# One matmul per group of keys stands half a loop step earlier on TensorE: graph network kernel, first edge stage

## The reference

```
h = relu(layernorm(x)); x = x + L0(h)   # segment sum of edge_attr_32 by src, two dense layers, batch norm
h = relu(layernorm(x)); x = x + L1(h)   # gather features[src], message per edge, scatter-add by dst
h = relu(layernorm(x)); x = x + L2(h)   # 3 rounds: segment_sum(norm * out[row], col), clipped
h = relu(layernorm(x)); x = x + L3(h)   # 3 rounds: segment_sum(wn * z[src], dst), relu, batch norm
```

## Time and profile before

| | us |
|---|---|
| median of 3 runs | 3483.51 |
| lowest and highest run | 3475.79, 3485.16 |
| the profiled execution, its own time | 3486.41 |
| its span in the profile | 3484.7 |
| first stage in it, first turn to last matmul | about 82 to 1006 |
| POOL's first add, last add, first gather | 222.06, 1021.88, 1058.52 |

### The profile page before, as it was taken

The page is one execution under the profiler, slowest core; times in us unless marked ns, Lnnn a source line. Parts: engine busy times, 40 slices in busy tenths (PEclk is TensorE's granted clock), DMA queues, the critical chain, the costliest instruction groups (busy, mean ns, idle before and its releaser), DMA issues. The chain is left out here.

```text
span 3484.7 us, 69264 instructions
## 1 busy us (share of the span) xinstructions
PE 2978.0 (85%) x19702; PEld 2385.9 (68%) x19703; DVE 2742.2 (79%) x5981; ACT 2291.3 (66%) x3192; POOL 2104.3 (60%) x1629
## 2 busy tenths in 40 slices
PE   3788788888877999999999999999999976657656
PEld 3677677777766888888888888888888841114256
DVE  6678888888877999999999999999999973450064
ACT  3678587877847888888888888888888832230000
POOL 4037888888866777777777777777777720000000
PEclk9999799899988999999999999999999987798878
DMA  9953222222213333333333333333333369999830
GB/s 402 422 188 36 12 15 16 14 15 15 15 6 67 52 50 52 52 52 50 52 52 51 52 52 52 50 52 52 51 51 52 52 242 426 425 389 377 362 139 6
DMA packets 265841, 397.89 MB, mean 114 GB/s; under 512 B 149901, under 2 KB 200836, under 8 KB 259252
## 3 DMA queue, kind: packets, MB, share of 16 engines
q0 software_dynamic: 149184, 124.54, 21.1%
q1 hardware_dynamic: 100180, 199.71, 16.9%
q10 hardware_dynamic: 16416, 72.92, 5.1%
HBM read 264.96 MB, written 132.05 MB: 114 GB/s over the span
## 5 line engine op out<-in xcount | busy, mean ns | idle before, releaser
L577 POOL DMA_INDIRECT both<-kept x782 | 1295.9, 1657 | 443.4 <-issue 205.1
L916 PEld LDWEIGHTS ps<-prod,big 128*128 128x128 f32 x7840 | 1134.3, 190 | 136.8 <-DVE prod L1283 133.2
L916 PE MATMUL ps<-prod,big 128*128 128x170 f32 x7840 | 1183.2, 310 | 22.2 <-DVE prod L1283 16.7
L585 POOL DMA_INDIRECT kept<-feat_dram,kept x782 | 760.8, 973 | 279.8 <-issue 232.2
L907 PE MATMUL ps<-prod,onehot 128*128 128x320 f32 x3920 | 719.4, 339 | 133.5 <-ACT onehot L665 116.2
L660 ACT ACTIVATE big<-iota_b,kept 128x640 f32<-128x640 f32 x1029 | 779.0, 815 | 13.6
L907 PEld LDWEIGHTS ps<-prod,onehot 128*128 128x128 f32 x3920 | 639.6, 207 | 167.9 <-issue 121.1
L665 ACT ACTIVATE big<-big 128x2560 f32<-128x2560 f32 x196 | 458.1, 2337 | 275.3 <-PE ps L916 275.2
L981 PE MATMUL ps<-w2mix,kept 65*128 65x384 f32 x1568 | 559.3, 500 | 21.6 <-ACT kept L712 21.6
L1455 DVE TENSOR_REDUCE kept<-kept 128x80 f32<-128x1280 f32 x392 | 562.0, 1474 | 0.0
L981 PEld LDWEIGHTS ps<-w2mix,kept 65*128 65x128 f32 x1568 | 284.1, 191 | 179.7 <-issue 23.5
(11 more groups left out here) (232 smaller groups left out, 2988.8 us busy)
## 6 DMA issues: line engine op xcount, KB each, us to landing
both<-big POOLq DMA_DIRECT2D x40, 2000.0 KB, 96.2
big<-both SPq DMA_DIRECT2D x50, 1600.0 KB, 10.7
adj_w<-kept ACTq DMA_DIRECT2D x32, 800.0 KB, 33.3
big<-adj_w SPq DMA_DIRECT2D x32, 800.0 KB, 12.1
big<-adj_w ACTq DMA_DIRECT2D x32, 800.0 KB, 11.7
kept<-keys_dram SPq DMA_DIRECT2D x196, 128.0 KB, 3.0
kept<-in_wT SPq DMA_DIRECT2D x196, 128.0 KB, 3.0
adj_c<-kept ACTq DMA_DIRECT2D x42, 400.0 KB, 32.5
```

Of the source, the lines that this page charges most:

```text
L577: pool.indirect_dma_start(both, bass.IndirectOffsetOnAxis(ap=sc_idx[:, c:c + 1], axis=0), sc_val[:, c // 2, c % 2, :], None, compute_op=AL ...
L585: pool.indirect_dma_start(gath[:, s % 2, k, :], None, feat_dram, bass.IndirectOffsetOnAxis(ap=src_i[:, 4 * s + k:4 * s + k + 1], axis=0)). ...
L916: mm = pe.matmul(part_sums(part, MSG), onehot[:, q, k, part * P:(part + 1) * P], prod[:, q, k, 0:HI * MSG], start=False, stop=False, skip_ ...
```

## The change

`spread_keys` for the next group but one stands in the even step, between the step's second and third chunk behind the hop, where it was in the odd step behind `merge_open`. It is the same 98 matmuls with the same two waits; the group's number and its slot are the same as well, only the place is one step earlier. No other engine's instructions move.

```
@@ phase0 on PE @@
                     merge_hop(g, slot, 2)
                 elif not is_last(s):
                     merge_open(g, slot)
-                if k4 % 2 and not is_last(s, 4):
-                    spread_keys(g + 1, 1 - slot)
+                if k4 % 2 == 0 and not is_last(s, 4):
+                    spread_keys(g + 2, slot)
                 scatter0(s, k4, 2)
                 scatter0(s, k4, 3)
```

## The result

The change made the kernel no faster: median 3492.18 us (20 runs) against 3482.40 us before (20 runs), ratio 1.0025 with a 95% interval of 1.0016 to 1.0034. Forecast were 3453 us. The single times spread more than before: 3478.15 to 3502.60 us, against 3475.79 to 3488.98. The profiled execution is the shortest of its twenty, 3478.15 us with a span of 3476.4 us; a second profile, of an execution of 3497.36 us, stands with the experiments.

The account below looks back on a forecast made before the run. A cycle of waits among PE, ACT and DVE paced the first stage. Its 43 us gain met POOL's limit, 34.8 - 3 - 1 = 31 us: 3486.4 - 31 = 3455.4, adjusted for the profiled run's 2.9 us above median to 3453; range 3446 to 3470.

Parts of the forecast that it names:

- the one at the seam: Where the first stage's adds end and the second stage's gathers begin: adds lengthen by 3 us in all.
- The cap: POOL's queue of first-stage adds, ahead of the first gather, limits the whole gain to 31 us; chance 0.60.
- The sign that the prediction had named for this: First-stage adds on POOL taking over 2.1 us each would show the forecast limit on the gain to be wrong.
- The 1 us in the same sum: At the second stage's start: 1 us taken off the gain for the first gather's data behind the adds.
- The ring is cut: First stage: the earlier spread ends ACT's waits for it, 0.88 and 2.31 us in the turn read.
- The added wait at nothing: PE's spread, now in the even step, waits for ACT's earlier squares: no cost, 1.6 us away from biting.
- The moved spread hidden by PE's wait for products: Even step on PE: the spread's 0.31 us cost nothing; at most 30 us without that cover.
- The clock: First stage: PE clock falls, 2.5 us each, drop from 0.47 of the turns to a fifth.
- The stage's gain: First stage: 37.5 turns become shorter by 43 us in all, at least 18 and at most 62 us.
- the clock as before: Rival, first stage: PE clock falls as often, gain 18 us, 3465 us; with cases between, 3456 to 3470, chance 0.25.
- The new wait: Rival, even step: PE held for ACT's squares, 41 us slower, 3525 us; chance 0.08 together with more clock falls.
- Nothing happens: Rival, first stage: DVE's turn stays at 17.48 us, its instructions lengthened beside POOL's adds; 3483 us, chance 0.07.

Follow-up runs that it names:

- the halves: Changed kernel with each first-stage DVE product made by two half-length instructions: 3467.79 us, 0.9939 of the kernel before; the same edit on the kernel before: 1.0009.
- the late spread: Changed kernel with the spread at the end of the even step, behind its last hop, not ahead of the third chunk: 3490.27 us, 1.0008 of the kernel before.

## Why the prediction was wrong

**The step that failed** is the one at the seam, in these words: "The adds will not keep their time quite ... I add 3 us, most of one such meeting." The cap had been recognised and was the bound, but its term was 3 us where 28.3 us were measured in the first profile (last add ends 1051.7, not 1023.4) and 40.3 us in the second (1063.7). I had treated 2.04 us an add as POOL's own, and counted only the meetings at the seam; it held 0.15 us of meetings for each add, and this share rests on where in DVE's turn the adds begin. At the seam the meetings stayed as they were (6.2 and 5.8 us behind the last spread); the growth lay in the stage, and waits for landings came on top. The sign that the prediction had named for this came: the adds took (1051.7 - 220.8) / 392 = 2.12 us each, over its 2.1. That the adds are the bound is shown by leaving 40 of them out in both kernels, and by moving six; that DVE's instructions stretch them, by the halves. The page of the Trainium skill that the prediction weighed, "SBUF — State Buffer", section "Who interferes with whom", has the one that comes second fully blocked, whichever it is, where the two share ports; the trace agrees for adds that start inside a DVE instruction (the rows of 603.55 and 608.38), and not for the product that starts inside an add (1.49 us as ever, 612.66). The prediction's estimate from it, 4 us by DVE's larger share of the time, was too small: DVE's busy time rose only from 469 to 483 in 569 us, while the meetings went from 0.15 to 0.21 us an add.

**The 1 us in the same sum** (34.8 - 3 - 1), for the first gather's data behind the adds: no run shows it. DVE's first instruction behind the gathers starts 6.3 to 6.5 us after the first gather in the seven profiles in which adds stand right ahead of it, and 7.0 to 7.3 us in the seven in which POOL had been idle.

**The ring is cut:** right. ACT's wait for line 865 has vanished, PE's for line 665 too.

**The added wait at nothing:** right; no wait at line 865. The 3.0 us to landing in that step are of another load (rows 10 are `keys_dram`, the load of rows 9 is `parts_dram`), which did no harm.

**The moved spread hidden by PE's wait for products:** wrong, with next to no effect on the time (1.0008 for the late spread, 1.0025 for the changed kernel). The spread stands one whole step, a quarter of a turn, sooner (the title's half step is a slip). The forecast looked at PE's next step only; the hop behind the spread is what DVE waits for ahead of its entries. 17.85 us a turn instead of 17.0; with the spread behind the hop 16.97. The price of a spread, 0.31 us, was taken as hidden; it was 0.42. The last 61 spreads take 535.5 us in the changed kernel (424.6 to 960.1) and 510.1 with the late spread (412.0 to 922.1), so the 60 half turns between them lose 25.4 us of the stage's gain, out of the 40 us by which the late spread has the table's load issued sooner (988.2 against 1028.1); 12.6 us of the rest lie ahead of these spreads, 2 us behind them.

**The clock:** direction right, extent too careful: no fall at all from 421 to 985, where I had taken a fifth of the turns.

**The stage's gain:** 43 us forecast, 23.8 us measured in the first profile, 28 us in the second, less for the longer turn and more for the clock. With the late spread the table's load came 63.7 us sooner than before the change (988.22), near the 62 us of the forecast's upper bound.

**The rivals:** the clock as before: no. The new wait: no. "Nothing happens" named the right pair of engines, DVE's instructions beside POOL's adds, but laid the price on DVE; the growth fell on POOL. DVE's one-hots of line 1304 do get longer beside adds, but hardly more than before: 0.60 us each on average from 421 to 960, and 0.59 before.

**What stays open:** why the adds begin at worse places of DVE's instructions now (0.57 us left of line 1309 on average where 0.15 us were left before). Both engines run at their own pace and each meeting shifts the next, so the pattern can be read off a trace but was not forecast; no run here sets it. The larger spread of the times, and the median 10 us above that of the kernel before, are only partly explained: 12 of 19 us between two profiles by the queue, the rest behind the second stage, where no run looks for the cause.

## What to carry to other kernels

When a change frees an engine that waits, look for the in-order queue with the least to spare at the next seam, and price that queue's own instructions under the new timing: a duration that contains meetings with another engine is no constant. A queue that "never waits" and has 35 us of slack over 800 us is within 5% of being the bound, and a cap that lies so close deserves bounds from both sides, like any other term. And of a moved instruction, ask for every consumer behind it, not only for the engine that it moves on.

## What the runs showed of the hardware

An indirect DMA issue on POOL (line 577, 1.54 us by itself) that starts while one of DVE's longer instructions runs is longer by what is left of that instruction less 0.13 us: 0.99 us with 1.12 us left (product), 0.48 us with 0.61 left (subtraction of line 1309). Of the 47 adds of the changed kernel that start in a product from 421 to 960, 44 follow this to within 0.01 us; the other 3 start with the product, 1.52 us before its end, and pay nothing. It is no matter of two inputs: in the one-hots of line 1304, which read one large operand, 0.33 us come with 0.46 left.

Where a product starts second, neither gets longer (1.54 and 1.49 us at 612.55; the products that start during an add take 1.49 us on average). A one-hot that starts during an add can: alone it takes 0.55 us, and 71 of 332 took over 0.62 us, up to 0.85. So POOL pays in meetings with products, and either of the two in meetings with one-hots.

An add behind an odd chunk's add, on whose landing it waits, starts 2.13 us behind it where 0.30 us are usual between adds.
